# Row records turned on chip instead of stored and loaded, and block sums stored in longer runs

## The chip, the cores and the metric

One core of one Trainium2 chip runs the whole program. The metric is device time in microseconds: 3159.52 us is the median of three runs of the kernel before (3158.77 to 3161.25).

## The reference

A graph attention layer and a mixture-of-experts layer act on 6250 nodes of 256 features (8 heads of 32), with 200000 edges sorted by their target node `dst`. Cut to what matters:

```python
h = (layernorm(x) @ W.T).reshape(n, H, D)
alpha = sum(h[src] * a_src) + sum(h[dst] * a_dst)         # for each edge and head
alpha += sum(relu(edge_attr @ edge_W.T + edge_b) * h[dst])
alpha = where(alpha >= 0, alpha, 0.2 * alpha)
ex = exp(alpha - segment_max(alpha, dst)[dst])
attn = ex / segment_sum(ex, dst)[dst]
x = x + segment_sum(h[src] * attn, dst) + bias
x = x + moe_ffn(layernorm(x))                             # two experts of eight
```

## The kernel before, in words

A prologue projects the nodes and writes for each a row of 272 floats (h, and its products with a_src and a_dst) to DRAM. It also sorts the edges into rows of four slots (W = 4) that share a target. 128 rows are a block; there are 440 blocks, in four groups of 128, 128, 128 and 56. For each row a record of five words says which source nodes its four edges have and which target row it belongs to, counted from the block's first target. `make_rows_of` makes a group's records on VectorE with the block on the partition, in `ro` (block, row, word). `store_table` and `store_attrs` store them, with the flags, the places (the row's target place, once more) and the edge attributes, to DRAM.

The edge loop takes four blocks a step (Q = 4), 110 steps, written out straight. In it the row lies on the partition, so that `load_rows` reads the stored records back transposed: 128 x 4 pieces of 20 bytes into `rec_in`, a ring of four steps. A step q runs so:

- SP (`load`, `store`, `body` in the sync block) sends, in this order, records, places, attributes (three times), four windows of node rows, and flags of step q + 2, and then the store of the sums of step q - 1. The sums of four blocks, [128, 4, 264], go to DRAM block by block: 512 pieces of 1056 bytes. Each of SP's waits holds all that is behind it on SP.
- POOL (`gather`, L1005) gathers the source rows of a step: 16 indirect DMAs of 128 rows, four for each block, with a column of `rec_in` as indices. The group for block b waits for the near copy of the block before it.
- PE (`body`): `turn_rows` transposes the tops of the scores (L1051); `front` makes the encoded attributes (L1038) and picks each row's target (L1045) with the one-hot matrix hotT; `add_up` sums the weighted rows of a block (L1067); `turn_back` is L1056.
- ACT (`body`): `make_hotT` turns the loaded places into hotT in two instructions (L1121 into places, L1125 into hotT); `make_hot` makes the other one-hot matrix with word W of the record as its bias (L1110, L1114); `move_near` copies the picks out of PSUM (L1134), `move_sums` the sums (L1155), `weights` takes the exponential (L1142, L1143).
- DVE (`body`): `scores` starts with raw (L1220), which waits for all 16 gathers of its step, and ends with row_top (L1228); `front` multiplies and reduces (L1208, L1212); `scan` runs the segment maxima; `fall` is L1246; `weigh` is L1258. After each of the first 19 steps of a group `expand` prepares a piece of the next group's table.

The semaphores between them are counted. After the loop the sums of blocks that share a target are merged and stored back, and the epilogue gathers the sums of each node tile (L1644) by an address that `prepare_merge` and `merge_blocks` work out; it then runs the experts.

Of the kernel before, what the change touches and what calls it, by code (L numbers as in the profile page):

```python
# [116 lines left out]
def store_table(nc, scr, b0, n, ro, flags, places, stored):  # L117
# [55 lines left out]
def make_rows_of(nc, x, words, base, base_mod, t, ro, flags, item, last_ok):  # L173

    x.wait()
    nc.vector.tensor_scalar(ro[:, :, 0:W].bitcast(I32), words.rearrange("p (r k) -> p r k", k=W), (1 << SRC_BITS) - 1, DUMMY,
                            ALU.bitwise_and, ALU.bitwise_xor)
    heads = words.rearrange("p (r k) -> p r k", k=W)[:, :, 0]
    near, ok, place, new = t["near"][:, :], t["ok"][:, :], t["place"][:, :], t["new"][:, :]
    nc.vector.tensor_scalar(ok, heads, float(1 << VALID_AT), None, ALU.is_ge)  # L180
# [8 lines left out]
    nc.vector.tensor_scalar(ro[:, :, W], place, -1.0, 1.0, ALU.mult, ALU.add)  # L189
# [21 lines left out]
def prologue(nc, a, scr, keep):  # L211

    with Scope(nc) as m:
# [25 lines left out]
        ro = m.sb("ro", [P, P, W + 1])  # L239
# [82 lines left out]
        def _(sp):  # L322
# [47 lines left out]
            store_table(nc, scr, 0, P, ro, flags, small["place"], s["table_stored"])  # L370
# [8 lines left out]
            sp.wait_ge(s["table_stored"], 64)  # L379
# [3 lines left out]
        def _(pool):  # L383
# [22 lines left out]
            nc.gpsimd.iota(keep["even_i"][:, :], pattern=[[0, 1]], base=1, channel_multiplier=1).then_inc(s["merge_consts"], 1)  # L406
            nc.gpsimd.iota(keep["own"][:, :], pattern=[[P, ITILES]], base=OUTSCR, channel_multiplier=1,
# [3 lines left out]
            nc.gpsimd.iota(keep["node_id"][:, :], pattern=[[P, NT]], base=0, channel_multiplier=1,  # L411
# [5 lines left out]
            pool.wait_ge(s["merge_consts"], 7)  # L417
# [43 lines left out]
            pool.wait_ge(s["merge_consts"], 9)  # L461
# [327 lines left out]
EXPANDED = 4 * WAY_BITS + 7 + 5  # L789
# [3 lines left out]
ROWS_RING = 4  # L793
# [7 lines left out]
def edge_loop(nc, a, scr, keep):  # L801

    with Scope(nc) as m:
        rec = m.sb("rec_in", [P, ROWS_RING, Q, W + 1])
        rec_i = rec[:, :, :, :].bitcast(I32)
# [6 lines left out]
        places = m.sb("places", [P, RING, Q, P])  # L812
# [20 lines left out]
        last_new = m.sb("last_new", [P, GROUPS])  # L833
        turned = m.sb("l_words_turned", [P, SLOTS], I32)
        moved = m.sb("l_moved", [P, SLOTS], I32)
        ro = m.sb("l_ro", [P, P, W + 1])
        head_flags = m.sb("l_flags", [P, P])
        parts = m.sb("l_parts", [P, KA, SLOTS], BF16)
        small = {n: m.sb("l_rows_" + n, [P, P], dt) for n, dt in (("near", I32), ("ok", F32), ("place", F32), ("new", F32))}
# [12 lines left out]
        s_rec = [m.sem(f"s_rec_loaded{i}") for i in range(ROWS_RING)]  # L852
# [7 lines left out]
            weight own_weight weighted merge summed sums tops_kept moved rows_out attr_made table_stored item items_made items_stored""".split()  # L860
# [23 lines left out]
        def _(sp):  # L884
            def load_rows(q):
                if q.s >= ROWS_RING:
                    before = straight(q.s - ROWS_RING)
                    for b in range(Q):
                        sp.wait_ge(s_src[before.par][b], 16 * W * (before.turn + 1))
                    sp.wait_ge(s["hot"], Q * (before.s + 1))  # L890
                rows = scr["block_rows"].rearrange("(n q) (r w) -> n r q w", q=Q, w=W + 1)
                v = rows[q.s, :, :, :] if isinstance(q.s, int) else rows[bass.ds(q.s, 1), :, :, :].rearrange("o r q w -> (o r) q w")
                sp.dma_start(rec[:, q.s % ROWS_RING, :, :], v).then_inc(s_rec[q.s % ROWS_RING], 16)

# [28 lines left out]
            def store(q):  # L923
                sp.wait_ge(s["sums"], Q * q.s + Q)
                rows = scr["sums"][0:BLOCKS * P, :].rearrange("(n q p) e -> n p q e", q=Q, p=P)
                v = rows[q.s, :, :, :] if isinstance(q.s, int) else rows[bass.ds(q.s, 1), :, :, :].rearrange("o p q e -> (o p) q e")
# [14 lines left out]
            def store_group(i, n):  # L941
                b0 = i * P + P
                sp.wait_ge(s["rows_out"], i + 1)
                store_table(nc, scr, b0, n, ro, head_flags, small["place"], s["table_stored"])
# [31 lines left out]
            for i in range(GROUPS - 1):  # L976
                for u in range(turn):
                    if u == LOADED_AT:
                        sp.wait_ge(s["table_stored"], 64 * (i + 1))
# [12 lines left out]
        def _(pool):  # L992
            def gather(q):
                pool.wait_ge(s_rec[q.s % ROWS_RING], 16 * (q.s // ROWS_RING + 1))
                nc.gpsimd.sem_inc(s["waited_by_pool"], 1)
                for b in range(Q):
                    if q.since(RING):
# [27 lines left out]
        def _(pe):  # L1025
# [21 lines left out]
            def turn_rows(q):  # L1047
                pe.wait_ge(s["row_top"], q.s + 1)
# [46 lines left out]

            for b in range(Q):
# [5 lines left out]
        def _(act):  # L1102
            def make_hot(q, b):

                n = q.s * Q + b
                if b == 0:
                    act.wait_ge(s_rec[q.s % ROWS_RING], 16 * (q.s // ROWS_RING + 1))
                if b or q.since(1):
                    act.wait_ge(s["hot"], n)
                nc.scalar.activation(apart[:, :], keep["node_at"][:, :], ACT.Abs, bias=rec[:, q.s % ROWS_RING, b, W:W + 1]).then_inc(s["apart"], 1)  # L1110
# [5 lines left out]
            def make_hotT(q):  # L1116
# [82 lines left out]
        def _(dve):  # L1199
# [82 lines left out]
            def prepare_merge():  # L1282
# [28 lines left out]
                nc.vector.tensor_scalar(gain[:, 1:BLOCKS], gain[:, 1:BLOCKS], float(P), None, ALU.add).then_inc(s["merge"], 1)  # L1311
# [3 lines left out]
                for t in range(ITILES):  # L1315
# [6 lines left out]
                                               spread(keep["later"][:, :], P), ALU.is_equal, ALU.mult).then_inc(s["merge"], 1)  # L1322
                dve.wait_ge(s["merge"], n + 5 + ITILES)
                nc.vector.tensor_tensor(away[:, :], away[:, :], ends[:, :], ALU.mult).then_inc(s["merge"], 1)
                dve.wait_ge(s["merge"], n + 7 + ITILES)
                nc.vector.tensor_tensor(to[:, :], away[:, :], own[:, :], ALU.add).then_inc(s["merge"], 1)
                dve.wait_ge(s["merge"], n + 8 + ITILES)

            def expand(i, k):
# [12 lines left out]
                elif k == 2 * WAY_BITS:  # L1342
                    if i:
                        dve.wait_ge(s["table_stored"], 64 * i)
# [680 lines left out]
```

## Time and profile before

| | |
|---|---|
| median of the runs | 3159.52 us (3158.77 to 3161.25) |
| profiled execution, span | 3570.8 us; the page gives no time beside it |
| PE, DVE, ACT, POOL busy | 69%, 64%, 29%, 53% |
| sums store, 110 issues | 528.0 KB each |
| places load, 110 issues | 256.0 KB each |
| windows load, 440 issues | 136.0 KB each |
| attributes load, 330 issues | 36.0 KB each |
| records load, 110 issues | 10.0 KB each |

The profiled execution is longer than the runs. Busy shares are of its span. PE's ends are modelled in the profile. The prologue ends near 177 us; the edge loop follows until about 3020 us; the merge and the epilogue take the rest.

### The profile page before, as it was taken

What the parts mean: (1) busy time and instruction counts of PE and PEld (TensorE: products, weight loads), DVE (VectorE), ACT (ScalarE), POOL (GpSimd) and SP (SyncE); (2) the same over time, 40 slices, a digit from 0 to 9 for tenths busy, and PEclk for the clock granted to TensorE, in tenths of its full rate; (3) what the DMA queues carried; (4) which work ended last, traced back from release to release, by engine and by line L of the source; (5) the groups of instructions that cost most, each with busy time, mean ns of one, the idle gap of its engine ahead of it and who ended that gap; (6) DMA issues with size and microseconds to landing.
All of it is one profiled execution on the core that took longest, in us unless ns stands there. A gap on an engine that the chain in (4) does not pass through costs nothing. (4 is left out here: it accounts for less than half of the span.)

```text
span 3570.8 us, 36328 instructions
## 1 busy us (share of the span) xinstructions
PE 2454.9 (69%) x8642; PEld 1654.1 (46%) x8642; DVE 2278.8 (64%) x3546; ACT 1022.1 (29%) x2822; POOL 1909.1 (53%) x2041
## 2 busy tenths in 40 slices
PE   1657676677677777776766767777766554269998
PEld 1424444444444444444444444444444332168887
DVE  7957767676667777776667777766666554251223
ACT  3522222222222222222222222222223221043332
POOL 3656566566566666666666665666666452607000
PEclk9857777777777777777777777777777676559999
DMA  8355555556555555556555555556556993310000
GB/s 269 122 140 145 153 145 153 145 148 178 143 157 146 154 147 149 155 143 177 141 158 147 153 155 142 157 146 175 153 145 147 124 122 57 87 28 3 19 19 31
DMA packets 341609, 471.12 MB, mean 132 GB/s; under 512 B 115596, under 2 KB 262718, under 8 KB 341170
## 3 DMA queue, kind: packets, MB, share of 16 engines
q0 software_dynamic: 90000, 262.14, 30.9%
q1 hardware_dynamic: 250578, 206.73, 20.0%
q8 instruction: 60, 0.98, 0.1%
q14 instruction: 123, 1.01, 0.1%
q10 hardware_dynamic: 848, 0.26, 0.0%
HBM read 380.17 MB, written 88.72 MB: 131 GB/s over the span
## 5 line engine op out<-in xcount | busy, mean ns | idle before, releaser
L1005 POOL DMA_INDIRECT src_in<-t_node_rows,rec_in x1760 | 1685.2, 957 | 1134.7 <-issue 549.0
L1067 PE MATMUL p_sum<-weighted,hot 128*128 128x264 f32 x3520 | 1287.9, 529 | 588.1 <-issue 384.4
L1067 PEld LDWEIGHTS p_sum<-weighted,hot 128*128 128x128 f32 x3520 | 893.7, 264 | 954.5 <-issue 631.7
L1208 DVE SCALAR_TENSOR_TENSOR prod<-p_enc,near 128x512 f32<-128x512 f32 x880 | 563.3, 681 | 382.9 <-ACT near L1134 328.9
L1258 DVE TENSOR_TENSOR weighted<-src_in,p_turn 128x1024 f32<-128x1024 f32 x440 | 534.5, 1215 | 309.8 <-ACT p_turn L1142 119.0
L1212 DVE TENSOR_REDUCE dots<-prod 128x32 f32<-128x1024 f32 x440 | 536.9, 1220 | 15.2
L1045 PE MATMUL p_pick<-win,hotT 128*128 128x272 f32 x880 | 383.6, 524 | 136.0 <-ACT near L1134 51.5
L1155 ACT COPY sums<-p_sum 128x264 f32<-128x264 f32 x440 | 164.5, 374 | 908.8 <-issue 403.2
L1134 ACT COPY near<-p_pick 128x272 f32<-128x272 f32 x440 | 169.9, 386 | 734.4 <-remote 383.4
L1038 PE MATMUL p_enc<-expander,attrT 30*128 30x256 bf16 x1760 | 321.2, 310 | 48.1 <-DMA attrT<-t_block_attr 36.8
L1045 PEld LDWEIGHTS p_pick<-win,hotT 128*128 128x128 f32 x880 | 154.7, 220 | 249.3 <-issue 179.8
L1038 PEld LDWEIGHTS p_enc<-expander,attrT 30*128 30x128 bf16 x1760 | 175.0, 122 | 200.3 <-issue 130.7
L1697 PE MATMUL p_up<-x2T,w 128*128 (+2 forms) x800 | 174.9, 377 | 9.5 <-DMA b<-in_L_ffn_b 9.5
L1110 ACT ACTIVATE apart<-node_at,rec_in 128x128 f32<-128x128 f32 x440 | 175.8, 400 | 0.0
L1707 PE MATMUL p_y<-w,act_h 128*128 128x256 f32 x784 | 173.1, 379 | 0.0
L1697 PEld LDWEIGHTS p_up<-x2T,w 128*128 128x128 f32 x800 | 150.7, 192 | 29.8 <-DMA b<-in_L_ffn_b 9.6
L1894 DVE TENSOR_TENSOR acc<-acc,p_y 128x256 f32 (+1 forms) x49 | 20.7, 422 | 218.1 <-PE p_y L1707 218.1
L1707 PEld LDWEIGHTS p_y<-w,act_h 128*128 128x128 f32 x784 | 148.9, 190 | 20.2
L1114 ACT ACTIVATE hot<-apart 128x128 f32<-128x128 f32 x440 | 136.2, 310 | 14.0
L1142 ACT ACTIVATE p_turn<-below 128x128 f32<-128x128 f32 x110 | 30.8, 280 | 372.6 <-remote 136.3
L1774 ACT ACTIVATE act_h<-p_up,b 128x256 f32<-128x256 f32 (+1 forms) x200 | 92.0, 469 | 158.1 <-PE p_up L1697 157.1
L1220 DVE TENSOR_TENSOR raw<-dots,src_in 128x128 f32<-128x128 f32 x110 | 31.7, 288 | 150.9 <-DMA src_in<-t_node_rows,rec_in 98.8
(334 smaller groups left out, 1674.1 us busy)
## 6 DMA issues: line engine op xcount, KB each, us to landing
win<-t_node_rows SPq DMA_DIRECT2D x440, 136.0 KB
t_block_sums<-sums SPq DMA_DIRECT2D x110, 528.0 KB
places<-t_block_places SPq DMA_DIRECT2D x110, 256.0 KB
src_in<-t_node_rows,rec_in POOLq DMA_INDIRECT x1760
attrT<-t_block_attr SPq DMA_DIRECT2D x330, 36.0 KB
t_node_rows<-out_rows SPq DMA_DIRECT2D x49, 136.0 KB, 1.7
x<-in_x SPq DMA_DIRECT2D x4, 1536.0 KB, 25.6
out_x<-x SPq DMA_DIRECT2D x48, 128.0 KB
```

The source lines that it names most:

```text
L1005: pool.indirect_dma_start(src[:, q.par, b, k, :], None, scr["rows"], bass.IndirectOffsetOnAxis(ap=rec_i[:, q.s % ROWS_RING, b, k:k + 1], a ...
L1038: last = nc.tensor.matmul(p_enc[(PAIRS * b + half) % len(p_enc)][:, j, :], slots, keep["expander"][:, :], start=True, stop=True)
L1045: nc.tensor.matmul(p_near, hotT[:, q.par, b, :], win[:, q.par, b, :], start=True, stop=True).then_inc(s["picked"], 1)
L1067: last = nc.tensor.matmul(p_sum[b % 2][:, 0:ROW], hot[:, q.par, b, :], weighted[:, b, k, :], start=(k == 0), stop=(k == W - 1))
L1110: nc.scalar.activation(apart[:, :], keep["node_at"][:, :], ACT.Abs, bias=rec[:, q.s % ROWS_RING, b, W:W + 1]).then_inc(s["apart"], 1)
L1134: nc.scalar.copy(near[:, q.par, b, :], p_near).then_inc(s["near"], 1)
L1155: nc.scalar.copy(sums[:, q.par, b, :], p_sum[b % 2][:, 0:ROW]).then_inc(s["sums"], 1)
L1208: nc.vector.scalar_tensor_tensor(prod[:, 2 * half:2 * half + 2, :], p_enc[(PAIRS * b + half) % len(p_enc)][:, :, :], 0.0, near[:, q.par, b ...
L1212: nc.vector.tensor_reduce(dots[:, q.par, b, :, :].rearrange("p k h -> p (k h)"), prod[:, :, :].rearrange("p k (h d) -> p (k h) d", h=H), A ...
L1258: nc.vector.tensor_tensor(heads(weighted[:, b, :, 0:D]), heads(src[:, q.par, b, :, 0:D]), spread(p_weight[:, b, :, :], HD), ALU.mult).then ...
L1697: last = nc.tensor.matmul(p_up[n % 4][:, 0:cols], w1[:, k, i, f * P:(f + 1) * P], x, start=(i == 0), stop=(i == 1))
L1707: last = nc.tensor.matmul(p_y[u][:, :], act_h[:, b, n, u * P:(u + 1) * P], w2[:, k, f, :], start=(n == 0), stop=(n == TOPK * hidden - 1))
```

## The change

`ro` is laid out (block, word, row) and kept for the whole edge part; its source numbers are turned into floats by one more copy. In the edge loop TensorE transposes each of its five words ([128 blocks, 128 rows] to [128 rows, 128 blocks]) and VectorE copies the result out of PSUM, into `row_src` and `row_near`, two buffers by group. For the first group this stands ahead of the loop, for the other three at the steps 19 to 23 of the group before. POOL's indices and ACT's bias are columns of these. `load_rows` and the stored records are gone. SP's order of loads is attributes, windows, places, flags. The places are loaded straight into hotT, once the picks of the step before last are done, and ACT's two instructions work there in place. The sums of a step are stored as they lie, 4 x 264 floats for each partition, and the addresses for items and node tiles follow the new order of rows (row of block b at p * 4 + b of its step).

```diff
@@ store_table @@
-    nc.sync.dma_start(scr["block_rows"][block, :], ro[0:n, :, :].rearrange("p r w -> p (r w)")).then_inc(stored, 16)
@@ make_rows_of @@
-    nc.vector.tensor_scalar(ro[:, :, 0:W].bitcast(I32), words.rearrange("p (r k) -> p r k", k=W), (1 << SRC_BITS) - 1, DUMMY,
-                            ALU.bitwise_and, ALU.bitwise_xor)
+    x.link(nc.vector.tensor_scalar(ro[:, 0:W, :].bitcast(I32), words.rearrange("p (r k) -> p k r", k=W), (1 << SRC_BITS) - 1, DUMMY,
+                                   ALU.bitwise_and, ALU.bitwise_xor))
+    x.wait()
+    nc.vector.tensor_copy(ro[:, 0:W, :], ro[:, 0:W, :].bitcast(I32))
@@ edge_loop, sync @@
-            def load_rows(q):
...
-                sp.dma_start(rec[:, q.s % ROWS_RING, :, :], v).then_inc(s_rec[q.s % ROWS_RING], 16)
@@ load_places @@
-                    sp.wait_ge(s["hotT"], q.prev().s)
+                    sp.wait_ge(s["picked"], Q * q.prev().s)
-                sp.dma_start(places[:, q.par, :, :].rearrange("p q r -> p (q r)"), v.broadcast_to([P, Q * P])).then_inc(s_places[q.par], 16)
+                sp.dma_start(hotT[:, q.par, :, :].rearrange("p q r -> p (q r)"), v.broadcast_to([P, Q * P])).then_inc(s_places[q.par], 16)
@@ store @@
-                rows = scr["sums"][0:BLOCKS * P, :].rearrange("(n q p) e -> n p q e", q=Q, p=P)
-                sp.dma_start(v, sums[:, q.par, :, :]).then_inc(s_stored[q.par], 16)
+                rows = scr["sums"][0:BLOCKS * P, :].rearrange("(n p q) e -> n p (q e)", q=Q, p=P)
+                sp.dma_start(rows[q.s, :, :], sums[:, q.par, :, :].rearrange("p q e -> p (q e)")).then_inc(s_stored[q.par], 16)
@@ load @@
-                load_rows(q)
-                load_places(q)
                 load_attr(q)
                 load_windows(q)
+                load_places(q)
                 load_flags(q)
@@ gather @@
-                pool.wait_ge(s_rec[q.s % ROWS_RING], 16 * (q.s // ROWS_RING + 1))
+                group, first = divmod(q.s, turn)
+                if first == 0:
+                    pool.wait_ge(s["rows_turned"], (W + 1) * (group + 1))
...
-                                                bass.IndirectOffsetOnAxis(ap=rec_i[:, q.s % ROWS_RING, b, k:k + 1], axis=0)
+                                                bass.IndirectOffsetOnAxis(ap=row_src[:, group % 2, k, at_block:at_block + 1], axis=0)
@@ edge_loop, tensor @@
+            def turn_table(group, k):
+                if group:
+                    pe.wait_ge(s["rows_out"], group)
+                if group or k:
+                    pe.wait_ge(s["rows_turned"], (W + 1) * group + k)
+                nc.tensor.transpose(p_turn[:, P:2 * P], ro[:, k, :], keep["ident"][:, :]).then_inc(s["rows_up"], 1)
             def body(q, ahead=2):
+                group, u = divmod(q.s - RING, turn)
+                pe.wait_ge(s["row_top"], q.s + 1)
+                if 0 <= group < GROUPS - 1 and 0 <= u - TURNED_AT <= W:
+                    turn_table(group + 1, u - TURNED_AT)
                 turn_rows(q)
...
+            for k in range(W + 1):
+                turn_table(0, k)
@@ make_hotT @@
-                of = places[:, q.par, :, :].rearrange("p q r -> p (q r)")
+                of = hotT[:, q.par, :, :].rearrange("p q r -> p (q r)")
                 nc.scalar.activation(of, of, ACT.Abs, scale=-1.0, bias=keep["after_p"][:, 0:1]).then_inc(s["far"], 1)
-                if q.since(RING):
-                    act.wait_ge(s["picked"], Q * q.prev().s)
-                nc.scalar.activation(hotT[:, q.par, :, :].rearrange("p q r -> p (q r)"), of, ACT.Relu, scale=-1.0, bias=1.0).then_inc(s["hotT"], 1)
+                nc.scalar.activation(of, of, ACT.Relu, scale=-1.0, bias=1.0).then_inc(s["hotT"], 1)
@@ edge_loop, vector @@
+            def keep_turned(group, k):
+                dve.wait_ge(s["rows_up"], (W + 1) * group + k + 1)
+                turned_to = row_src[:, group % 2, k, :] if k < W else row_near[:, group % 2, :]
+                nc.vector.tensor_copy(turned_to, p_turn[:, P:2 * P]).then_inc(s["rows_turned"], 1)
@@ expand @@
+                elif 0 <= k - TURNED_AT <= W:
+                    keep_turned(i + 1, k - TURNED_AT)
@@ merge_blocks @@
-            nc.vector.tensor_tensor_scan(past[:, :], sum_row[:, :], sum_row[:, :], 0.0, ALU.add, ALU.max).then_inc(s["past"], 1)
+            nc.vector.tensor_tensor_scan(past[:, :], sum_row[:, :], keep["before"][:, 0:1].broadcast_to([NT, P]), 0.0, ALU.add, ALU.add).then_inc(s["past"], 1)
```

## Rows read from the trace of the kernel before

**Rows 1.** By stretch: us; PE, PEld, DVE, ACT, POOL busy; clock; DMA share; GB/s.

```profile
400.00:2700.00 2300.00, 1636.50 (x5342) 1033.29 (x5343) 1637.39 (x2313) 650.40 (x1935) 1413.04 (x1474) 0.75 0.56 153
2770.00:2980.00 210.00, 117.17 (x380) 74.24 (x378) 105.66 (x145) 45.85 (x136) 102.66 (x109) 0.70 0.91 120
3100.00:3570.00 470.00, 402.71 (x1884) 359.53 (x1884) 152.98 (x481) 161.59 (x331) 85.17 (x117) 0.86 0.08 24
```

**Rows 2.** Order of time: start us, us, instruction, [idle before <- releaser].

```profile
1251.49 2.02 PE L1067 MATMUL p_sum<-weighted,hot 128*128 128x264 f32 x8
...
1258.14 0.28 ACT L1142 ACTIVATE p_turn<-below 128x128 f32<-128x128 f32 x1 [5.65 <-remote]
```

**Rows 3.** DVE's waits, 400 to 2700 us: us, times, longest.

```profile
DVE prod L1208 <- ACT near L1134: 261.3, 154, 4.0
DVE weighted L1258 <- ACT p_turn L1142: 104.5, 47, 5.6
...
DVE raw L1220 <- issue: 50.1, 27, 3.5
...
DVE raw L1220 <- DMA src_in<-t_node_rows,rec_in: 23.3, 12, 3.7
```

**Rows 4.** PE's waits at L1051, same stretch.

```profile
PE p_turn L1051 <- issue: 64.0, 41, 3.8
...
PE p_turn L1051 <- DVE row_top L1228: 27.3, 11, 3.5
```

**Rows 5.** Order of time, one step with the store ahead of the last gather.

```profile
934.74 0.38 SPq L927 DMA_DIRECT2D t_block_sums<-sums  x1
...
935.30 0.39 SPq L893 DMA_DIRECT2D rec_in<-t_block_rows  x1
...
935.73 0.93 SPq L914 DMA_DIRECT2D places<-t_block_places  x1
...
936.66 0.95 POOL L1005 DMA_INDIRECT src_in<-t_node_rows,rec_in  x1 [0.30 <-issue]
...
942.84 0.29 DVE L1220 TENSOR_TENSOR raw<-dots,src_in 128x128 f32<-128x128 f32 x1 [3.46 <-issue]
```

**Rows 6.** DMA share (last but one column) of one microsecond of that step.

```profile
938.00:939.00 1.00, 1.00 (x3) 0.43 (x2) 1.00 (x2) 0.00 (x0) 0.86 (x1) 0.50 1.49 160
```

**Rows 7.** Order of time, one step with the store beside the last gather.

```profile
1835.01 0.95 POOL L1005 DMA_INDIRECT src_in<-t_node_rows,rec_in  x1 [0.30 <-issue]
...
1835.27 0.38 SPq L927 DMA_DIRECT2D t_block_sums<-sums  x1
...
1839.25 0.29 DVE L1220 TENSOR_TENSOR raw<-dots,src_in 128x128 f32<-128x128 f32 x1
```

**Rows 8.** DVE's waits in the last steps, 2770 to 2985 us.

```profile
DVE raw L1220 <- DMA src_in<-t_node_rows,rec_in: 64.0, 6, 14.3
```

**Rows 9.** Order of time, start of the edge loop.

```profile
189.41 0.51 SPq L914 DMA_DIRECT2D places<-t_block_places  x1
...
192.05 3.71 SPq L921 DMA_DIRECT2D win<-t_node_rows  x4
193.47 0.72 ACT L1121 ACTIVATE places<-places,after_p 128x512 f32<-128x512 f32 x1 [7.22 <-DMA places<-t_block_places]
...
194.76 0.37 ACT L1134 COPY near<-p_pick 128x272 f32<-128x272 f32 x1
...
195.93 0.95 POOL L1005 DMA_INDIRECT src_in<-t_node_rows,rec_in  x1 [7.33 <-ACT near L1134]
```

**Rows 10.** Order of time, tight step: last window issue, ACT's use of places.

```profile
1652.69 0.34 SPq L921 DMA_DIRECT2D win<-t_node_rows  x1
...
1661.10 0.70 ACT L1121 ACTIVATE places<-places,after_p 128x512 f32<-128x512 f32 x1
```

**Rows 11.** PE's transposes at L1669: ns min/median/max, first and last start.

```profile
L1669 PE MATMUL p_T<-ident,acc x98: 417/433/478, 3119.4 to 3195.0; 128*128 128x128 f32 x98
```

**Rows 12.** Groups by line, DVE: busy us, mean ns of one, idle before.

```profile
L1246 DVE TENSOR_TENSOR below<-score,p_turn 128x128 f32<-128x128 f32 x110 | 30.8, 280 | 0.0
```

More of the change, by code:

```diff
@@ L114, in sem, with store_table @@
         return self.enter_context(self.nc.semaphore(name))
-def store_table(nc, scr, b0, n, ro, flags, places, stored):
+def store_table(nc, scr, b0, n, flags, places, stored):
     block = bass.ds(b0, n) if not isinstance(b0, int) else slice(b0, b0 + n)
-    nc.sync.dma_start(scr["block_rows"][block, :], ro[0:n, :, :].rearrange("p r w -> p (r w)")).then_inc(stored, 16)
     nc.sync.dma_start(scr["block_flags"][block, :, :], flags[0:n, :].unsqueeze(1).broadcast_to([n, H, P])).then_inc(stored, 16)
@@ L369, in _ @@
             sp.wait_ge(s["rows_out"], 1)
-            store_table(nc, scr, 0, P, ro, flags, small["place"], s["table_stored"])
+            store_table(nc, scr, 0, P, flags, small["place"], s["table_stored"])
             sp.wait_ge(s["attr_made"], 1)
@@ L833, in edge_loop @@
         last_new = m.sb("last_new", [P, GROUPS])
+        lane = m.sb("lane", [P, 1])
+        sum_row_at = m.sb("sum_row_at", [P, GROUPS])
         turned = m.sb("l_words_turned", [P, SLOTS], I32)
         moved = m.sb("l_moved", [P, SLOTS], I32)
-        ro = m.sb("l_ro", [P, P, W + 1])
+        ro = keep["ro"]
+        row_src = m.sb("row_src", [P, 2, W, P], I32)
+        row_near = m.sb("row_near", [P, 2, P])
         head_flags = m.sb("l_flags", [P, P])
         parts = m.sb("l_parts", [P, KA, SLOTS], BF16)
-        small = {n: m.sb("l_rows_" + n, [P, P], dt) for n, dt in (("near", I32), ("ok", F32), ("place", F32), ("new", F32))}
+        small = {n: m.sb("l_rows_" + n, [P, P], dt) for n, dt in (("near", I32), ("ok", F32), ("place", F32))}
+        small["new"] = head_flags
         last_of = m.sb("last_of", [ITILES - 1, 1])
@@ L859, in edge_loop @@
         names = """waited_by_pe waited_by_pool ones_set apart hot far hotT picked near enc prod dots raw full score row_top rowT run tops back below
-            weight own_weight weighted merge summed sums tops_kept moved rows_out attr_made table_stored item items_made items_stored""".split()
+            weight own_weight weighted merge summed sums tops_kept moved rows_out rows_up rows_turned attr_made table_stored item items_made items_stored""".split()
         s = {n: m.sem("l_" + n) for n in names}
@@ L884, in _ @@
         def _(sp):
-            def load_rows(q):
[L886 to L892, printed above, removed]
-                sp.dma_start(rec[:, q.s % ROWS_RING, :, :], v).then_inc(s_rec[q.s % ROWS_RING], 16)
             def load_attr(q):
@@ L1105, in make_hot @@
                 n = q.s * Q + b
-                if b == 0:
-                    act.wait_ge(s_rec[q.s % ROWS_RING], 16 * (q.s // ROWS_RING + 1))
+                group, at_block = divmod(n, P)
+                if at_block == 0:
+                    act.wait_ge(s["rows_turned"], (W + 1) * (group + 1))
                 if b or q.since(1):
                     act.wait_ge(s["hot"], n)
-                nc.scalar.activation(apart[:, :], keep["node_at"][:, :], ACT.Abs, bias=rec[:, q.s % ROWS_RING, b, W:W + 1]).then_inc(s["apart"], 1)
+                nc.scalar.activation(apart[:, :], keep["node_at"][:, :], ACT.Abs, bias=row_near[:, group % 2, at_block:at_block + 1]).then_inc(s["apart"], 1)
                 act.wait_ge(s["apart"], n + 1)
@@ L1310, in prepare_merge @@
                 dve.wait_ge(s["merge"], n)
-                nc.vector.tensor_scalar(gain[:, 1:BLOCKS], gain[:, 1:BLOCKS], float(P), None, ALU.add).then_inc(s["merge"], 1)
+                nc.vector.tensor_scalar(gain[:, 1:BLOCKS], gain[:, 1:BLOCKS], float(Q), 1.0, ALU.mult, ALU.add).then_inc(s["merge"], 1)
                 nc.vector.tensor_copy(even[:, :], even_i[:, :]).then_inc(s["merge"], 1)
@@ L1361, in make_items @@
                 y.link(nc.vector.tensor_scalar(item[:, :, 1], item[:, :, 1], -1.0, None, ALU.add))
-                nc.vector.tensor_copy(item_i[:, :, 0], keep["row_at"][:, :]).then_inc(s["items_made"], 1)
+                y.link(nc.vector.tensor_scalar(keep["lane_i"][:, :], keep["lane_i"][:, :], Q - 1, None, ALU.bitwise_and))
                 y.wait()
+                y.link(nc.vector.tensor_copy(lane[:, :], keep["lane_i"][:, :]))
+                y.wait()
+                y.link(nc.vector.scalar_tensor_tensor(sum_row_at[:, :], lane[:, 0:1].broadcast_to([P, GROUPS]), 1.0 - P, keep["row_at"][:, :],
+                                                      ALU.mult, ALU.add))
+                y.wait()
+                nc.vector.tensor_copy(item_i[:, :, 0], sum_row_at[:, :]).then_inc(s["items_made"], 1)
                 y.link(nc.vector.tensor_tensor(last_new[:, :], item[:, :, 1], item[:, :, 0], ALU.not_equal))
@@ L1390, in _ @@
             x = Chain(dve, s["moved"])
+            for k in range(W + 1):
+                keep_turned(0, k)
             for b in range(Q):
```

45 lines of the change are left out of this document (21 added, 24 removed).

## The prediction

> **What bounds the kernel now.** I began with the page's span, then took the edge loop by stretches, then who waits for whom on each engine, and last single steps in order of time. The profiled execution spans 3570.8 us (the table of times), and the page gives no other time for it; the runs' median is 3159.52 us. So every sum below is made against 3570.8 us and then scaled by 3159.52 / 3570.8 = 0.885. That scaling is an assumption: no row says which stage carries the 411 us between the two.
>
> The loop holds most of the time. POOL's 1474 instructions between 400 and 2700 us are 92 steps of 16 gathers, so a step takes 25.0 us, and there are 110. In this even middle, 400 to 2700 us, no engine is full by its own rows: PE is busy 1636.5 of 2300 us, DVE 1637.4, POOL 1413.0, and the granted clock is 0.75, a mix of the two levels of 1.2 and 2.4 GHz [rows 1]. PE is nearer to full than its rows say. Eight p_sum matmuls are drawn as 2.02 us from 1251.49 us, and yet ACT's exponential, which waits for them and for DVE's difference, starts only at 1258.14 us, after 5.65 us of idling [rows 2]. I read that as PE working at its lower clock behind its drawn ends. So a step is a ring: gather of a step's source rows (POOL, 16 issues), scores (DVE), transposed tops and picks (PE), near copies (ACT), gather of the next step. Which link is last changes from step to step.
>
> POOL is the link closest to a fixed price: 1413.0 us / 1474 = 959 ns for an issue [rows 1] and 0.30 us of gap [rows 5], so 16 x 1.26 = 20.1 us a step. Then the last gather has to land before raw can start. DVE waits there 50.1 + 23.3 = 73.4 us in the middle, 39 times, 1.9 us each [rows 3]. PE in turn waits 64.0 + 27.3 = 91.3 us for what follows from it, its transpose p_turn at L1051 [rows 4]. That is the only place in the ring where I can see the DMAs. In the last seven steps they bind outright: DMA share 0.91 [rows 1], and raw waits 64.0 us for the gathers [rows 8].
>
> **Why the last gather lands late.** In the step at 934 us the sums store (528 KB) is issued at 934.74, the row records at 935.30, the places (256 KB) at 935.73, and POOL's last gather of the step at 936.66, done at 937.61. Raw starts at 942.84, 5.2 us after that and after 3.46 us of idling [rows 5]. In the microsecond from 938 the DMA share is 1.49 [rows 6]. In another step the store is issued only 0.7 us before the last gather is (1835.27 against the end at 1835.96) and raw follows it after 3.3 us, without idling [rows 7]. So SP's burst, sent as soon as the sums are out, coincides with the landing on which the step hangs, and costs it at least 1.9 us there.
>
> **The change, part by part.**
>
> *Row records no longer stored and loaded.* One of SP's transfers per step goes, 512 pieces of 20 bytes, from just behind the store. It is 10 KB, so by bytes nothing; by pieces it is as many as the store has. Its instruction blocks SP 0.39 us in the example and the places issue behind it 0.93 us [rows 5].
>
> *Places behind the windows.* 256 KB leave the moment right after the store, and come about 8 us later, when only the next step's first gathers are in flight. What can be late in exchange is hotT on ACT, and behind it the picks on PE and every near copy. In a tight step the last window issue ends at 1653.03 and ACT needs the places at 1661.10 [rows 10]: 8.1 us, against 3.6 us that a places load took from issue end to use at the start (189.92 to 193.47) [rows 9]. Hidden, with 4 us left; if that cover were gone, each microsecond would cost 110.
>
> *Store as 4224-byte runs.* Same bytes, 128 pieces and not 512. Between nothing and a quarter of the time it holds the engines; I take a little.
>
> *Together:* the landing gets shorter by 0 (the store's bytes alone decide) to 1.9 us (the whole difference to the other step). I take 1.0, half way, since no row is nearer to one end: the 256 KB of places leave the burst, and attrT (3 x 36 KB) and the first window (136 KB) move up. At 1.0 us, the 39 waits, or 43 over the 2558 us from 212 to 2770 us, give at most 43 us; waits shorter than 1 us give less, so 35. PE's 91.3 us show that nearly all of it reaches the ring, but steps in which PE lags at the lower clock will swallow some: 0.8, so **-28 us**. Both ends: 0 and -82 (73.4 x 2558 / 2300, all waits gone).
>
> Here the Trainium skill speaks against the change ("DMA: Bandwidth & Descriptors", section "Queues, rings and completion order"): an engine serves its rings in turn, but drains a whole packet of descriptors from one before it switches. By that the store would hold a gather for its 528 KB however it is cut, and the first term would be the records and places alone. The share above 1 in the burst does not contradict it, and no row separates the two.
>
> *Start of the loop.* Here the order costs. Before, places for step 1 are issued at 189.41, ACT takes them up at 193.47 for its two hotT instructions and only then copies near (194.76), on which POOL's second group of gathers hangs (195.93) [rows 9]. After, SP sends attrT, windows (their last issue ended at 195.76), places: two records and the places of step 1 leave the way, 0.5 us each, so its windows end 1.4 us sooner, at 194.3, the places issue at 194.8, ACT takes them up 3 to 3.6 us later, and needs 193.47 to 194.76, 1.3 us, until near. Near at 199.3 and not 194.8: **+4.5 us**, from 3 to 6. The five first turns (PE transpose and DVE copy by turns, 0.43 + 0.28 us and two handovers, an estimated 0.9 us each) delay only POOL's first group of gathers, behind which POOL idles 7.33 us anyway [rows 9].
>
> *Turning in the loop.* 15 steps get a PE transpose of 128x128 (433 ns for the epilogue's like ones [rows 11]) ahead of p_turn, and a DVE copy out of PSUM (280 ns for the like one [rows 12]) ahead of the next raw: 6.5 + 4.2 = 10.7 us if all of it is on the ring, 0 if none. Half of the steps wait elsewhere: **+5.5 us**.
>
> *Small things.* One copy of 128x512 for each of four groups (four times the elements of the 280 ns one, so at most 1.1 us [rows 12]), four tiny operations for the items, one in the merge, a scan's operand: +4 us at most if none had cover, against a store of 320 KB less at the end of the prologue. ACT and POOL drop a wait that had long been satisfied. PE waits for row_top one instruction earlier, with nothing between. In the last seven steps the DMA engines lose the records and gain nothing else, at most -2 us; but SP's burst behind the item loads makes one late places load later, up to +4. Taken as **0**.
>
> Sum: -28 + 4.5 + 5.5 = -18 us of 3570.8, times 0.885 is -16: **3143 us**.
>
> **Rivals.**
>
> *A, slower.* The landing is not shortened, as the store alone holds the engines and attrT and windows fill the gap. For it: the store is the largest transfer of the burst and stays 528 KB. Against: the places are half as large again. [...] Then only the costs stand: 4.5 + 5.5, up to 4.5 + 10.7 + 4, so +9 to +17 scaled, 3168 us at its centre (3168.4), 3176 at its end. It decides once the landing gains under 0.25 us (10 us over 43 waits).
>
> *B, no difference.* The gather lands sooner, but PE, at its lower clock and behind its drawn ends, is late next and gives back two thirds: -28 becomes -10, which the costs cancel: 3159 us. For it: PE at 0.75 of clock with 71% drawn busy; DVE waits for near and for the weights, both behind PE, for far longer (261.3 + 104.5 us [rows 3]) than for the gathers. Against: PE itself waits 91 us where raw's lateness arrives.
>
> *C, far faster.* All waits at raw go, and PE, with fewer gaps, is granted the higher level more: -82 + 10 = -72, scaled -64: 3096 us. For it: in the epilogue, where PE is drawn busy 402.7 of 470 us, it is granted 0.86 [rows 1]. Against: the windows' 544 KB still run into some landing.
>
> **How the numbers follow.** This kernel's times differ by 0.08%; I call anything within 0.2% (6.3 us) the same. Forecast 0.44, A 0.22, B 0.24, C 0.10. Faster is the forecast and C: 0.54; same 0.24; slower 0.22. The range leaves out 2 in 10: below, half of C, so 3100; above, the end of A, 3178.
>
> **What would show it.** After: no row for rec_in; places issued behind the windows; in the middle, DVE's waits at raw down from 73 us to about 35 to 40, and PE's at p_turn with them; a step of about 24.8 us; first near 4 us after 194.76; transposes of 0.43 us at three places of five steps. Raw waits unchanged, with the step longer, is A. Raw waits down and near or p_sum waits up by as much is B. A granted clock clearly over 0.75 is C. I would be wrong altogether if ACT came to wait for places in every step, or if POOL's issue itself (959 ns) changed.

## The result, and the profile after

| | us | ratio to before |
|---|---|---|
| before, beside it | 3159.14 (3157.46 to 3161.25) | |
| after | 3082.05 (3077.06 to 3085.36) | 0.9742 [0.9716, 0.9767] |
| forecast | 3143 (3100 to 3178) | 0.995 |

The change gains 77 us where I forecast 16, and the time lies outside my range. It came out nearest to rival C (3096 us), with costs and gains that were not C's, as the runs below show.

Whole executions of either kernel come at two heights of mean granted clock, 0.81 to 0.84 and 0.75 to 0.77; the profile that the prediction was made from is of the lower one (3570.8 us), the timed runs are of the upper one (3159 us), and every ratio below is of runs taken together at one height. The first two answers are of the changed kernel, one execution at either height: span and clock.

```profile
core 0: 3080.8 us, clock 0.831
```

```profile
core 0: 3522.4 us, clock 0.768
```

Now the even middle of the loop, 400 to 2300 us, at the upper height; first the kernel before (a second profile of it, 3140.76 us of time), then the kernel after (its first profile). These are the columns of [rows 1].

```profile
400.00:2300.00 1900.00, 1437.21 (x5207) 907.01 (x5206) 1589.90 (x2246) 638.25 (x1887) 1372.12 (x1438) 0.84 0.65 180
```

```profile
400.00:2300.00 1900.00, 1471.21 (x5375) 935.63 (x5374) 1638.18 (x2341) 656.66 (x1937) 1417.20 (x1480) 0.85 0.64 185
```

POOL's count gives the step: 1900 x 16 / 1438 = 21.1 us before, 1900 x 16 / 1480 = 20.5 us after. In [rows 1] it was 25.0. POOL's own price of a step, 16 x (0.957 + 0.30), stays 20.1 us, so before had 1.0 us a step above it, and after has 0.4.

The waits in the same stretch (us in all, times, longest) show where the 0.6 us went. Before:

```profile
DVE raw L1220 <- DMA src_in<-t_node_rows,rec_in: 152.1, 79, 4.2
...
DVE prod L1208 <- ACT near L1134: 42.3, 75, 1.1
...
PE p_turn L1051 <- DVE row_top L1228: 189.9, 86, 4.4
```

After, the answers to [rows 3] and [rows 4]:

```profile
DVE raw L1226 <- DMA src_in<-t_node_rows,row_src: 82.4, 48, 5.3
DVE prod L1214 <- ACT near L1140: 71.1, 126, 1.1
...
PE p_turn L1044 <- DVE row_top L1234: 92.5, 76, 3.3
...
PE p_turn L1069 <- DVE row_top L1234: 29.3, 15, 4.8
```

Raw waits for the last gather in 79 of 90 steps before, and in about half of them after. That is 1.7 us a step before (152.1 us in 90 steps) and 0.9 us after (82.4 us in 93). Not all of the difference reaches the step: prod waits 29 us more for ACT's near copies.

One step in order of time says why. Before, SP's burst (store, records, places) goes out while POOL issues the last two gathers of the step, and raw starts 4.7 us after the last of them is issued (1181.30 + 0.95), having idled for 1.05 us:

```profile
1180.13 0.38 SPq L927 DMA_DIRECT2D t_block_sums<-sums  x1
1180.69 0.37 SPq L893 DMA_DIRECT2D rec_in<-t_block_rows  x1
1181.11 0.72 SPq L914 DMA_DIRECT2D places<-t_block_places  x1
...
1181.30 0.95 POOL L1005 DMA_INDIRECT src_in<-t_node_rows,rec_in  x1 [0.31 <-issue]
...
1186.94 0.29 DVE L1220 TENSOR_TENSOR raw<-dots,src_in 128x128 f32<-128x128 f32 x1 [1.05 <-DMA src_in<-t_node_rows,rec_in]
```

After, the places follow the store by 7.1 us, when raw has run, and raw (1159.73) starts 2.9 us after the last gather of its step is issued (1155.86 + 0.95), without idling:

```profile
1153.75 0.33 SPq L919 DMA_DIRECT2D t_block_sums<-sums  x1
1154.12 1.28 SPq L894 DMA_DIRECT2D attrT<-t_block_attr  x3
...
1155.86 0.95 POOL L999 DMA_INDIRECT src_in<-t_node_rows,row_src  x1 [0.31 <-issue]
...
1157.10 3.69 SPq L914 DMA_DIRECT2D win<-t_node_rows  x4
...
1159.73 0.31 DVE L1226 TENSOR_TENSOR raw<-dots,src_in 128x128 f32<-128x128 f32 x1
1160.84 0.43 SPq L907 DMA_DIRECT2D hotT<-t_block_places  x1
```

Over all steps between 400 and 2300 us, counting 16 gathers to a step, raw starts on average 4.8 us after the last one is issued before the change (c0), and 3.8 us after it with the change.

The start of the loop in the kernel after, the answer to [rows 9]:

```profile
195.68 0.43 SPq L907 DMA_DIRECT2D hotT<-t_block_places  x1
...
199.11 0.72 ACT L1129 ACTIVATE hotT<-hotT,after_p 128x512 f32<-128x512 f32 x1 [4.75 <-DMA hotT<-t_block_places]
...
200.40 0.37 ACT L1140 COPY near<-p_pick 128x272 f32<-128x272 f32 x1
201.57 0.94 POOL L999 DMA_INDIRECT src_in<-t_node_rows,row_src  x1 [10.00 <-ACT near L1140]
```

### The profile page after: what moved, and what is told of

Same layout as the page of the kernel before. It is cut to its first block and busy times, and to the rows that moved or that the text cites. A ratio compares the mean times of both kernels' runs of the same rounds, so it can differ in the third digit from the quotient of the medians.

```text
span 3080.8 us, 35752 instructions
## 1 busy us (share of the span) xinstructions
PE 2268.7 (74%) x8662; PEld 1543.3 (50%) x8662; DVE 2279.0 (74%) x3574; ACT 1027.7 (33%) x2822; POOL 1908.0 (62%) x2042
## 5 line engine op out<-in xcount | busy, mean ns | idle before, releaser
L999 POOL DMA_INDIRECT src_in<-t_node_rows,row_src x1760 | 1683.7, 957 | 687.9 <-issue 498.7
L1060 PE MATMUL p_sum<-weighted,hot 128*128 128x264 f32 x3520 | 1113.1, 471 | 356.7 <-issue 251.2
L1060 PEld LDWEIGHTS p_sum<-weighted,hot 128*128 128x128 f32 x3520 | 787.0, 232 | 670.4 <-issue 358.4
L1039 PE MATMUL p_pick<-win,hotT 128*128 128x272 f32 x880 | 371.7, 509 | 34.2 <-ACT hotT L1131 22.1
L1032 PE MATMUL p_enc<-expander,attrT 30*128 30x256 bf16 x1760 | 314.6, 305 | 7.7 <-DMA attrT<-t_block_attr 7.4
L1917 DVE TENSOR_TENSOR acc<-acc,p_y 128x256 f32 (+1 forms) x49 | 20.6, 421 | 217.5 <-PE p_y L1730 217.5
L1118 ACT ACTIVATE apart<-node_at,row_near 128x128 f32<-128x128 f32 x440 | 176.4, 401 | 0.0
L1044 PE MATMUL p_turn<-ident,row_top 128*32 128x128 f32 x110 | 33.0, 300 | 166.9 <-DVE row_top L1234 166.9
```

The lines of the kernel that those rows point to most:

```text
L1032: last = nc.tensor.matmul(p_enc[(PAIRS * b + half) % len(p_enc)][:, j, :], slots, keep["expander"][:, :], start=True, stop=True)
L1039: nc.tensor.matmul(p_near, hotT[:, q.par, b, :], win[:, q.par, b, :], start=True, stop=True).then_inc(s["picked"], 1)
L1060: last = nc.tensor.matmul(p_sum[b % 2][:, 0:ROW], hot[:, q.par, b, :], weighted[:, b, k, :], start=(k == 0), stop=(k == W - 1))
```

## The experiments

The letter of a label says which runs were taken together. My first theory was the prediction's: SP's burst delays the last gather's landing, and the change thins it out. The rivals: the store's runs, the records' 512 pieces, or the places' position carries the gain.

### The change's parts at the lower clock

b0 is the kernel before. b1 is before with only the store (and its addresses) changed; b2 is after with the old store; b3 is after with the places back at the head:

```diff
 def load(q):                      # b3, and d2 below
+    load_places(q)
     load_attr(q)
     load_windows(q)
-    load_places(q)
     load_flags(q)
```

> The kernel before, unchanged, profiled once more, since its first profile spans 3570.8 us against runs of 3159 us, while the changed kernel's profile spans 3080.8 us against runs of 3082 us. If the first profile was an odd execution: span near 3158 us, step near 21.2 us, most of PE's and ACT's unexplained waits gone, granted clock over 0.76. If the profiler itself slows this kernel: span near 3570 us again.

> The kernel before with the store of 4224-byte runs alone (and the addresses that go with it). Theory 1 (the small pieces of SP's burst hold the last gather, the store's 512 pieces as much as the records' 512): about half of the 77 us, so 3110 to 3130 us. Theory 2 (bytes hold it, as forecast for the lesser part): within 10 us of 3159. Theory 3 (the store is all of it): 3080 us or less, since the start and the turning cost nothing here.

> The changed kernel with the store cut as before, 512 pieces of 1056 bytes (addresses to match, same instructions). Theory 1: 3110 to 3130 us. Theory 2 (records and the places' order carry the gain): within 10 us of 3082. Theory 3: 3159 us or more, as the costs of start and turning remain: up to 3185.

> The changed kernel with the places sent ahead of attributes and windows again (still straight into hotT). If the places' 256 KB behind the store held the last gather: 15 to 30 us longer than 3082. If their place matters only at the loop's start: 5 us shorter, 3077.

Measured, against before at 3535.18 us (b0 itself 3522.85): b1 0.9998 [0.9979, 1.0017], b2 0.9985 [0.9968, 1.0002], b3 0.9934 [0.9908, 0.9960]. The store alone changes nothing, the change without it gains nothing clear of noise, and putting the places back helps by 0.7%; why it helps here is open. That was a miss for every theory, and it sent me to the clocks: here a step takes 24.6 us, 4.5 us above POOL's price, so POOL and the landing are not what it waits for. The middle of b0 has the [rows 1] picture again:

```profile
400.00:2300.00 1900.00, 1353.09 (x4488) 851.63 (x4487) 1385.36 (x1957) 546.83 (x1627) 1189.96 (x1239) 0.75 0.57 155
```

### The same parts at the upper clock

c0 is before, c1 after, and c2 is after with a load of 512 pieces of 20 bytes (of node rows, into a tile that nobody reads) at the head of each step's loads. d1 is after with the old store, d2 is b3's kernel, d3 is b1's. d4 is the kernel before with one edit:

```diff
 def load(q):                      # d4
     load_rows(q)
-    load_places(q)
     load_attr(q)
     load_windows(q)
+    load_places(q)
     load_flags(q)
```

> The kernel before, profiled on this call's chip. The chip of the last call ran it in 3535 us at a granted clock of 0.76, the chip of the first comparison in 3159 us. If this chip is like the first: about 3159 us, clock 0.80 to 0.83, step 21.2 us, POOL's issues nearly without gaps. If like the second: about 3530 us, clock 0.76, step 25 us.

> The changed kernel, unchanged. On a chip like the first: 3082 us, ratio 0.974. On a chip like the last call's: theory 1 (POOL's issues bound the changed kernel only where PE is granted enough clock; else PE's clock does) gives a ratio of 0.990 to 1.000, near the 3511 us of the variant with the places first; theory 2 (the gain is the landing of the last gather, whatever the clock) gives 77 us there too, 3458 us.

> The changed kernel with a load of 512 pieces of 20 bytes a step put back at the head of SP's loads, into a tile that nobody reads. If those pieces behind the store are what held the last gather: half or more of the gain is lost (30 to 77 us over c1). If their bytes are all that counts: within 6 us of c1.

> The changed kernel with the store cut as before (512 pieces of 1056 bytes), once more, on a chip that grants 0.83 of the clock if this call gets one. The records' return cost nothing measurable there, so the store's pieces and the places' order are left. Theory S (512 pieces of the store hold the last gather longer than 128 do): about 3130 to 3145 us, step 21.0 to 21.1, waits of raw for its gathers back near 150 us in the middle 1900 us. Theory O (it is the places' 256 KB behind the store): 3070 to 3082 us, step 20.5. On a slow-clock chip both give under 0.5% of 3530.

> The changed kernel with the places ahead of attributes and windows. Theory O: step 21.0 to 21.1, 3130 to 3140 us, raw's waits near 150 us in the middle. Theory S: 5 us less than the changed kernel, from the loop's start alone, 3065 to 3077 us.

> The kernel before with the store of 4224-byte runs alone. Theory S: most of the gain, 3065 to 3095 us (no later start, no turning). Theory O: within 10 us of before. If the two share it: 3110 to 3130.

> The kernel before with the places sent behind the windows (own tile, records still first). Theory O: most of the gain less 5 us at the start, 3080 to 3100 us. Theory S: 5 us more than before, 3150 us or so. If the two share it: 3115 to 3135.

| | us | ratio | raw's waits, 400 to 2300 us |
|---|---|---|---|
| c1 after | 3070.41 | 0.9769 [0.9734, 0.9804] | 87.7 (54) |
| c2 records' pieces back | 3077.75 | 0.9800 [0.9759, 0.9842] | 83.2 (55) |
| d1 old store | 3081.22 | 0.9789 [0.9771, 0.9808] | 81.7 (49) |
| d2 places first | 3160.76 | 1.0059 [1.0037, 1.0082] | 159.9 (80) |
| d3 before, store in long runs | 3144.55 | 0.9994 [0.9981, 1.0007] | 151.6 (81) |
| d4 before, places last | 3075.23 | 0.9765 [0.9745, 0.9786] | 89.3 (62) |

One line's move does it. d4, with the records, the old store and no turning, has the whole gain; d2, with everything but that line, has none of it and is slower than before. Both lines of raw, d2's and then d4's:

```profile
DVE raw L1226 <- DMA src_in<-t_node_rows,row_src: 159.9, 80, 3.7
```

```profile
DVE raw L1220 <- DMA src_in<-t_node_rows,rec_in: 89.3, 62, 3.1
```

The store's runs are nothing (d3), and 512 small pieces in the worst place cost no more than c2's interval lets one see. d2 is even slower than before, by 0.6%, with steps of 21.37 against 21.14 us in c0. Its places go out nearer to the store: with no records between them, the median places load is issued 0.8 us ahead of the step's last gather, in c0 0.2 us ahead (SP waits only 2.2 us in 1900 us for the picks). That fits the collision, but no run separates it from d2's other differences.

### Why the places' position counts

Three causes were left: their 256 KB, the 128 reads of one DRAM row of 2 KB, or SP's instruction ahead of the others. e1 and e2 are d2 with one edit each. e1 never loads the places and e2 leaves them stale after the first two steps, so both compute wrong picks and serve for timing alone.

```diff
-    sp.dma_start(hotT[...], v.broadcast_to([P, Q * P]))        # one row to 128 partitions
+    sp.dma_start(hotT[...], scr["block_flags"][0:P, 0:Q, :])   # e1: 128 different rows
+    sp.dma_start(hotT[..., 0:32], v[:, 0:32].broadcast_to([P, 32]))   # e2, from step 2 on
```

> The changed kernel with the places load back at the head of SP's loads, and read as 128 different rows of 2048 bytes (from the stored flags) in place of one row of 2048 bytes sent to 128 partitions. The same 256 KB, the same 128 pieces and the same place in time as in the run with places first (1.0059 of before). hotT holds no places, so the picks and all that follows from them are wrong. Theory bytes (256 KB in the burst hold the last gather's landing, wherever they are read): 1.002 to 1.010, raw's waits for the gathers near 150 us in 400 to 2300 us. Theory one row (128 reads of one DRAM row are what is slow): 0.975 to 0.982, raw's waits near 85 us, as with the places behind the windows. Theory issue (only SP's instruction ahead of attributes and windows counts): 1.002 to 1.010.

> The changed kernel with the places load back at the head of SP's loads, but after the first two steps with 32 of 512 floats: 128 pieces of 128 bytes, 16 KB and not 256 KB. hotT is left stale for the rest, so the picks are wrong. Theory bytes: nearly all of the gain of the order comes back, 0.975 to 0.981, raw's waits 80 to 95 us in 400 to 2300 us. Theory one row, if it is the number of reads of one row and not their bytes: 1.002 to 1.010. Theory issue: 1.002 to 1.010 too, since SP's instruction stays where it was; raw's waits near 150 us.

Measured: e1 3107.35 us, 0.9899 [0.9866, 0.9932]; e2 3081.06 us, 0.9808 [0.9778, 0.9838], beside before at 3142.47. From d2 (1.0059) to c1 (0.9769) there are 2.9 points. Other rows alone give back 1.6 of them, a sixteenth of the bytes 2.5. So SP's instruction is no cause that these runs can see; the bytes are, and about half of what they cost comes from reading one row 128 times. Theory bytes and theory one row each named one cause, and each was half right; theory issue fell. Two cautions: c1, d2 and the pair e1, e2 were not run side by side, and hotT holds other data in e1 and e2 (the clock in the middle is 0.84 in e1 and 0.83 in e2 and d2; whether the data has a part in it is not shown). e1 and e2 in the middle of the loop, raw's line:

```profile
DVE raw L1225 <- DMA src_in<-t_node_rows,row_src: 135.5, 72, 3.2
```

```profile
DVE raw L1227 <- DMA src_in<-t_node_rows,row_src: 117.0, 79, 5.4
```

The waits fall less than the time does in e2 (117.0 where c1 has 87.7 at nearly the same time), so the sum of one wait is not the whole price of a late landing. The time from the last gather's issue to raw, averaged over the same steps, orders the kernels as their step times do: 5.1 us in d2, 4.8 in c0, 4.6 in e1, 4.2 in e2, 3.7 in c1, at steps of 21.37, 21.14, 20.89, 20.62 and 20.48 us.

### Start, turning and the store's place

e3 is after with the places first for the first two steps only, and with the table's transposes at the end of PE's step; e4 is e3 with the store between windows and places.

```diff
 def body(q):                      # PE, e3
-    turn_table(group + 1, u - TURNED_AT)
     turn_rows(q)
...
     add_up(q, 1)
+    turn_table(group + 1, u - TURNED_AT)
 def body(q):                      # SP, e4 (wait for the sums of q - 2 ahead)
-    load(q + 2); store(q - 1)
+    load_attr(q + 2); load_windows(q + 2); store(q - 2); load_places(q + 2); load_flags(q + 2)
```

> The changed kernel, with places first for the first two steps alone (before the loop's first near copy) and last after that, and with the table's transposes on PE moved from ahead of p_turn to the end of the step, VectorE's copy one step later. Theory ring: the start gives back 5 us, and the 15 turned steps (20.8 against 20.4 us, the transposes ahead of the tops) give back 5 to 15: 3055 to 3062 us where the changed kernel has 3070, ratio 0.970 to 0.974. Theory POOL (16 issues of 0.957 us with gaps of 0.30 set the steps, so what PE is spared comes back as a wait for POOL): only the start counts, 0.975 to 0.977.

> The same as the run before it in this call, and the sums store sent behind the attributes and windows of the same burst, not ahead of them (order: attributes, windows, store, places, flags). Theory bytes: the store's 528 KB leave the last gather's landing as the places did; raw's waits fall from 88 us to 30 to 60 us in 400 to 2300 us, and a step from 20.4 us towards POOL's 20.1: 0.958 to 0.968. Theory POOL: the steps are at POOL's issue rate already, the waits at raw fall and others rise by as much: within 0.002 of the run before it. Theory windows (544 KB of windows now meet the landing in the store's place): no gain or slower, 0.972 to 0.985, raw's waits unchanged.

Measured: e3 3071.10, 0.9773 [0.9749, 0.9796]; e4 3060.95 (3053.79 to 3065.72), 0.9738 [0.9713, 0.9763]. e3's first raw comes at 211.6 us and not at 216.7 as in c1, but its middle steps are 20.52 and not 20.48, and of the 5 us nothing can be seen in the time. They are 0.16%, less than the half width of either interval, so neither the start nor the turning can be priced by e3. e4 is the fastest of its set, 10 us under e3, yet the theory behind it fell: raw's waits stay (84.0 us in 36 waits, against 82.1 in 47), as "theory windows" had it, while its time was a little shorter. Of the 10 us, 5.6 are in the last nine steps (251.0 against 256.6 us, one profile each). It was never run beside the changed kernel itself at this clock, so that it beats it stays open.

### The burst held until the landing

If what counts is whose bytes are under way while the last gather lands, then holding all of SP's burst until raw has run must take that wait away. g1 is the kernel after again; g2 and g3 are e3 with:

```diff
 def body(q):                      # SP
+    sp.wait_ge(s["raw"], q.s + 1)
+    load_attr(n); load_places(n); load_windows(n); load_flags(n)     # n = q + 2
+    store(q - 2)                  # g3: ahead of load_attr
```

> The changed kernel once more, so that the two kernels of this call can be compared with it on one chip: 0.974 to 0.978 of before, raw's waits for the gathers near 88 us in 400 to 2300 us.

> The kernel of e3_start_turn with SP's whole burst of a step held until raw has run, that is until the last gather of the step has landed: SP waits for raw of step q, then sends attributes, places, windows and flags of step q + 2 and the store of step q - 2. The same bytes, pieces and instructions as in the changed kernel. Theory collision (what counts is whose packets are on the engines while the last gather lands): raw's waits fall from 82 us to under 40 us in 400 to 2300 us, a step goes from 20.5 us to 20.1 to 20.3 us, POOL's pace, 0.962 to 0.971 of before. Theory bound elsewhere (the changed kernel's steps hang on POOL and on PE's clock already): within 0.002 of the changed kernel. Theory too late (about 14 us from raw to the first use of the step's attributes, places and windows, for 1.4 MB beside 2.2 MB of gathers): ACT waits for places and PE for windows, slower than the changed kernel.

> The same as the run before it in this call, but the store at the head of the burst, so 528 KB ahead of the places. Theory collision: as good as with the store last, within 0.002 of it, since no order inside the burst meets the last gather any more. Theory order (the order inside the burst counts by itself): slower than with the store last by 10 us or more, and the raw waits longer.

These runs came at the lower clock. Before 3526.95 us; g1 3521.41, 0.9992 [0.9973, 1.0010]; g2 3540.19, 1.0040 [1.0020, 1.0059]; g3 3540.05, 1.0035 [1.0018, 1.0052]. Raw's two lines in g1, then in g2:

```profile
DVE raw L1226 <- issue: 11.0, 10, 2.1
DVE raw L1226 <- DMA src_in<-t_node_rows,row_src: 7.8, 8, 1.6
```

```profile
DVE raw L1231 <- DMA src_in<-t_node_rows,row_src: 2.8, 2, 1.6
DVE raw L1231 <- issue: 1.4, 5, 0.5
```

18.8 us of waits become 4.2 (5.7 in g3, with the store first, so the order in the burst does not matter to it). That speaks for the collision as the cause of the wait, but does not show it: in g2 raw also starts later after the last issue (a median of 4.9 us against 4.4 in g1), and a later raw has less to wait for. In time it buys nothing here, since at this clock the wait isn't on the path. Why g2 is 0.4% slower is open. The issues of its windows stretch over 10 us, but no row between 400 and 2300 us has an engine waiting for a window; POOL waits longer for DVE's weighted (110.8 us against 82.1 in g1):

```profile
1183.95 10.77 SPq L914 DMA_DIRECT2D win<-t_node_rows  x4
...
1196.09 0.95 POOL L1004 DMA_INDIRECT src_in<-t_node_rows,row_src  x1 [4.51 <-DVE weighted L1269]
```

Whether it pays at the upper clock was not tried. And g1 says the most on the prediction: at the clock of its profile the change as a whole is worth 0.1%, between a gain of 0.27% and a loss of 0.1%, where the sum had 18 us of 3570.8, 0.5%.

## Why the prediction was wrong

**What failed is the step "Together".** It priced the landing at 1.0 us for 39 waits of [rows 3], 43 over the loop, and carried -28 us. Mechanism and direction were right: the places leave the burst, the last gather lands sooner, raw waits less. Even the 1.0 us was near: from the last issue to raw it is 4.8 us in c0 and 3.7 in c1. What was mis-sized is how many steps it counts in. At the clock of the timed runs raw waits in 79 of 90 steps, not 39 of 92, and 152.1 us in 1900 us, not 73.4 in 2300. From c0 to c1 64.4 us of it go in 1900 us, and 0.66 us a step (21.14 to 20.48) over the 94 steps from the fifth to the ninety-eighth is -62 us; the last nine steps add -7 and the start takes +2 (spans: -70).

The same step's factor of 0.8, for what reaches the ring, failed too, at the clock of the profile. There raw's waits fell from 58.9 us in b0 to 18.8 in g1, in 1900 us, which is more than I forecast, and the time hardly moved (0.9992).

**Why it was mis-sized: the opening assumption.** I scaled all by 3159.52 / 3570.8 and said that no row tells which stage carries the 411 us. The numbers did tell. It is hardly possible that the prologue up to 212 us and what follows the loop from 3020 us on (551 us) shrink by 411 us between them, so most of it had to be in the loop. If both keep their length, a step takes (3159.5 - 212 - 551) / 110 = 21.8 us, against 25.0 in the profile and 20.1 for POOL. A loop at 21.8 us hangs on POOL and on the landing behind it, and there each microsecond of landing is a microsecond of step. A loop at 25.0 us hangs on PE at its lower clock ([rows 2] show it waiting 5.65 us for PE), and there the same microsecond is covered. I scaled the waits down by 0.885 where they had to be scaled up by more than two. Had I priced the 1.0 us of the landing for every step, I would have had -110 + 10, and half of the steps -45: the measured 77 lies between.

**Which part gains.** I gave the gain to three parts together. *Records*: nothing to be measured, as I had it by bytes (c2). *Store in long runs*: "I take a little" was too much, 0.9994 in d3. The Trainium skill ("DMA: Bandwidth & Descriptors", "Queues, rings and completion order") states only that an engine takes its rings in turn, a packet of descriptors at a time. That the store then holds a gather for all its 528 KB, however it is cut, was my conclusion and does not follow from it. That the cut does not matter came true (d3); that the store's bytes could decide alone, the lower end of my term, is refuted by d4. *Places*: all of it, with about half of their price from reading one row 128 times, which I had not thought of.

**Places late on ACT** (4 us left): right in the middle of the loop, where neither ACT nor PE waits for places. From 2300 us on ACT waits 29.3 us for them in c1 and 8.9 in c0, and yet the last nine steps got 7 us shorter.

**Start of the loop**: +4.5 forecast, 3 to 6. Near comes at 200.40 and not at 194.76, +5.6, but in these two profiles the prologue differs by itself; from c0 to c1 near comes 1.9 us later (196.83 and 198.75) and the first raw 2.0 us. The order does cost more (near at 193.09 in d2 and 198.75 in c1, 5.7 us); the sum missed that the rest of the change gives some 3.7 us of it back (196.83 in c0, 193.09 in d2).

**Turning**: +5.5 forecast. The transposes took 401 ns and the copies 285 ns, as priced from [rows 11, 12]:

```profile
L1340 DVE CAST row_src<-p_turn 128x128 int32<-128x128 f32 x16 | 4.6, 285 | 1.7 <-PE p_turn L1069 1.7
...
L1252 DVE TENSOR_TENSOR below<-score,p_turn 128x128 f32<-128x128 f32 x110 | 30.8, 280 | 0.0
```

In c1 the 15 turned steps take 20.6 us on average and d4's like ones 20.4, so about +3 us, between my ends of 0 and 10.7 (one profile each, so no more than a hint). **Small things**: the one added copy takes 0.43 us for each group, under its bound.

**The rivals.** A and B did not come, as timed; B is what happens at the lower clock (0.9992), raw's waits gone and no time gained. That C came near in size is luck: raw's waits did not all go, they were twice as many as the profile showed, and 82 us are left. My sign for C, "a granted clock clearly over 0.75", did show (0.83), but it is the height of the execution and in the kernel before as well (c0: 0.828), no effect of the change. Read by that sign, the result would have confirmed a mechanism that wasn't there.

## What to carry to other kernels

When the profiled execution and the timed runs differ by a tenth, work out first which step time the timed runs must have, and price each wait at that step; the scale factor of the whole is not the scale factor of a wait. A transfer that nobody waits for still has a place in time: send it where no landing hangs on the queue, and look for that place before rewriting what it carries. Undo the order of the transfers as an experiment of its own, since here one moved line of a change of some hundred was all of it. That move paid only where the landing was on the path: with the places first, the changed kernel was 3 points slower at the upper clock (1.0059 against 0.9769) and no slower at the lower one (0.9934 against 0.9992, not run side by side).

## What was not expected of the hardware

- The same program on the same chip ran at a mean granted clock of 0.835 in c1 (3070 us) and 0.768 in g1 (3521 us). One matmul at p_sum is drawn with a mean of 467 and 522 ns there (400 to 2300 us), yet the step went from 20.5 to 24.6 us. What sets the height is not known.
- A load of 256 KB that reads one DRAM row 128 times costs about twice as much beside a gather as one that reads 128 rows, the same 128 in every step (1.0059 and 0.9899, where none in that place is 0.9769).
- 512 pieces of 20 bytes a step cannot be told from their absence (0.9800 against 0.9769, intervals overlapping), nor a store of 528 KB cut in 512 pieces from one cut in 128 (0.9994 [0.9981, 1.0007]).
